# Another order of work in a software-pipelined attention and product-key expert layer

## The chip, the cores and the metric

One core of a Trainium2 chip runs the whole kernel. The metric is the device time of one execution in microseconds; lower is better. Times of single steps come from the profile of one execution.

## What is computed

One transformer layer on x of shape (16, 512, 128), float32, with a layer norm behind each half:

```python
x = layernorm(x + attention(x))     # 16 heads of 8, causal, q and k RMS-normed and rotated
x = layernorm(x + experts(x))       # product keys
# attention: qkv = x @ w_qkv.T; softmax(q k^T * 8**-0.5, causal) @ v; @ w_proj.T
# experts:
xn = rmsnorm(x) * norm_w
q = (xn @ w_q.T).reshape(b, t, 8, 2, 128)
sim1, sim2 = q[..., 0, :] @ keys0, q[..., 1, :] @ keys1      # 32 keys a side
s1, i1 = top_k(sim1, 8);  s2, i2 = top_k(sim2, 8)
fs, pk = top_k(s1[..., :, None] + s2[..., None, :], 8)       # of 64 pairs
fi = take_along(i1 * 32 + i2, pk)                            # 1024 experts
hidden = gelu(xn . expert_down[fi]) * relu(fs)
out = sum_k hidden_k * expert_up[fi_k]
```

## The kernel before

The 16 batches of 512 positions (four tiles of 128, `NT`) pass through a software pipeline. Each engine has its own program with one `iteration`, whose order is written out by hand, and all engines meet only at semaphores. In iteration b the batch `b` has its scores, exponentials and attention sums; `nxt` = b+1 is loaded, projected, normalised and rotated; `late` = b-1 gets its output projection, the first norm, similarities and selection; `older` = b-2 its expert weights; `oldest` = b-3 its expert outputs and the second norm. Iterations 3 to 14 are a loop; the ones ahead and behind leave out what has no batch. Where an expert is picked, no gather is made: the kernel computes `hid` for all 1024 experts (`hidden_products` L877, Gelu in `hidden` L553) and multiplies it with weights that come from one-hot matrices.

- Scores and exponentials. An iteration has 40 steps on TensorE and ScalarE, four groups of four heads with ten units each (`scores` L804, `exps` L609). The results alternate between two PSUM banks by the list `S_ORDER`, which also has the projections `v`, `xT`, `qk` and the transposed q and k (`Q`, `K`); a step in the list waits until what stood two places before is read. `attend` (L821) sums a group's values, 32 float32 products into OV; it waits for all ten exponentials of the group, and the first exponential of the next group waits for it, since `prob` has one buffer. `attended` (L625) copies OV, `transpose_o` (L835) turns it, `normalise_o` (L1134) divides by the sums. In the kernel before, `attend` of a group stands behind the second unit of the next one.
- q and k. `taken_qk` (L566) squares and copies them, `squares_summed` (L1081) sums, `rotate` (L434, GpSimd) turns them, `normalise` (L1096) multiplies them by their inverse roots. Then they are split into bfloat16 parts: `first_parts` (L580, ScalarE), `rests` (GpSimd), `second_parts` (ScalarE), `third_parts` (GpSimd), and `transpose_stack` (L759) and `transposed` (L598) bring them into `qT`, `kT` at four steps, `QK_STEPS`.
- Norms. `norm1_moments` (L1157) and `norm2` (L1181) take moments; `roots` (L1092) finds all inverse roots of q, k and both norms together, eleven dependent steps with one-hots in between; `norm1` (L1171) makes `yi`, which `transpose_yi` (L869) turns for `project_similarities` (L858), at `SIMS_STEPS`. ScalarE copies them in `similarities` (L546).
- Selection. `top_keys` (L1198) takes the maxima and their places of a tile (16 MAX8 and 16 FIND_INDEX8), `candidates` (GpSimd, L463) the sums, `top_pairs` (L1213) the best eight and a mask `gat`, `gather` (GpSimd, L489) multiplies the mask with the numbers, `turn_numbers` (L888) and `transpose_selection` (L900) turn them, `decode` (L1236) splits the experts' numbers. `top_pairs` of tile 0 waits for both rotations, as `gat` lies on their buffer.
- Weights. `one_hot` (L1258) writes 8 of 256 rows, 32 such instructions a batch; `weighted_one_hots` (L1271) makes a quarter of the other factor, `weights` (L909) multiplies 24 small products a part, 32 parts of 4 a chunk, and `apply_weights` (L1294) multiplies a chunk into `hid`. `expert_outputs` (L932) uses `hid`.

All operators on an engine are in order: a wait on one holds whatever is queued behind it.

## Time and profile before

| | us |
|---|---|
| median of three runs | 1940.49 (1939.04 to 1941.27) |
| profiled execution | 1938.47 |
| its span | 1936.6 |
| one pass of the loop, from 1003.40 | 112.64 |
| the next, from 1116.04 | 112.64 |

| busy over the span | TensorE | its weight loads | VectorE | ScalarE | GpSimd |
|---|---|---|---|---|---|
| us | 1430.0 | 1024.8 | 1385.7 | 920.6 | 630.4 |
| share | 74% | 53% | 72% | 48% | 33% |

The loop's twelve passes lie from 327 to 1678.6 us and repeat each other. "Idle" in brackets behind an instruction is the time its engine stood before it, and the name after the arrow is the instruction whose semaphore ended that. TensorE's ends are modelled; starts are not. PE is TensorE, PEld its weight loads, DVE VectorE, ACT ScalarE, POOL GpSimd.

### The profile page before, as it was taken

How to read it: one execution, taken by the hardware profiler on the slowest of the kernel's cores; microseconds unless marked ns; L12 is line 12 of the kernel's file. 1: busy time of each engine (PE TensorE's matmuls, PEld its weight loads, DVE VectorE, ACT ScalarE, POOL GpSimd, SP SyncE). 2: the span in 40 equal slices, each digit the busy share in tenths (PEclk: the TensorE clock that was granted, in tenths of full speed). 3: DMA queues.
4: the chain of work that ended last, by engine and by line, in shares of the span. 5: the costliest groups of instructions: out<-in, count | busy, mean ns of one | idle time of the engine just before them, and what ended most of it. 6: DMA issues, size and time to landing. Idle time of an engine off the chain costs nothing.

```text
span 1936.6 us, 55124 instructions
## 1 busy us (share of the span) xinstructions
PE 1430.0 (74%) x21008; PEld 1024.8 (53%) x21008; DVE 1385.7 (72%) x6568; ACT 920.6 (48%) x1502; POOL 630.4 (33%) x1024
## 2 busy tenths in 40 slices
PE   3665787777787777777777777787777778786757
PEld 2333455455565645555564555555455555555556
DVE  4217776777877677787767778876777887677885
ACT  1765544544555454455545445554544455441201
POOL 2315241432624143262414326241432624122220
PEclk7697978888897988889798888989888898987766
DMA  2000000000000000000000000000000000000000
GB/s 71 6 6 7 7 8 7 13 3 7 13 7 13 7 13 2 11 9 7 13 7 13 2 15 5 7 13 7 13 2 18 2 2 13 2 13 2 7 2 14
DMA packets 29989, 18.81 MB, mean 10 GB/s; under 512 B 1824, under 2 KB 29216, under 8 KB 29728
## 3 DMA queue, kind: packets, MB, share of 16 engines
q1 hardware_dynamic: 29728, 15.23, 2.8%
q8 instruction: 176, 2.88, 0.7%
q14 instruction: 85, 0.70, 0.1%
HBM read 11.04 MB, written 4.19 MB: 8 GB/s over the span
## 4 chain that ended last, share of the span: by engine, by line
DVE 37%; PE 34%; ACT 12%; issue 12%; POOL 3%; SPq 0%; DVEq 0%; ACTq 0%; DMA 0%; POOLq 0%
DVE onehot L1264 10%; PE OV L829 8%; PE G L937 6%; DVE topi L1210 5%; PE G L926 4%; PE S L815 4%; DVE psel L1226 3%; DVE topv L1204 3%; ACT prob L623 3%; PE F L895 2%; DVE whot L1289 2%; ACT kT_odd L607 2%; PE F L865 2%; DVE fsel L1221 2%; PE S L755 1%
## 5 line engine op out<-in xcount | busy, mean ns | idle before, releaser
L623 ACT ACTIVATE prob<-S 128x512 f32<-128x512 f32 x640 | 369.9, 601 | 718.7 <-PE S L817 380.0
L926 PE MATMUL G<-whot,onehot 128*128 128x16 bf16 x12288 | 387.7, 171 | 89.1 <-DVE hid L1302 88.8
L926 PEld LDWEIGHTS G<-whot,onehot 128*128 128x128 bf16 x12288 | 371.3, 99 | 133.7 <-issue 98.6
L1264 DVE TENSOR_TENSOR onehot<-lo_no,elo 128x1024 bf16<-128x1024 uint16 x512 | 388.4, 814 | 0.0
L815 PE MATMUL S<-qT,kT_even 128*128 128x512 bf16 (+3 forms) x512 | 157.2, 334 | 122.8 <-ACT kT_odd L607 51.2
L817 PE MATMUL S<-causal,ident_b 128*128 128x128 bf16 x1024 | 210.9, 239 | 0.0
L1204 DVE MAX8 topv<-sims 128x8 f32<-128x32 f32 x1024 | 101.2, 175 | 145.1 <-ACT sims L550 145.0
L829 PE MATMUL OV<-prob,vp 128*9 128x512 f32 (+3 forms) x2048 | 191.0, 524 | 0.7 <-ACT prob L623 0.7
L815 PE MATMUL S<-qT,kT_odd 128*128 128x256 bf16 (+3 forms) x512 | 158.4, 336 | 44.2 <-ACT prob L623 33.5
L502 POOL COPY y<-y_new 128x512 f32<-128x512 f32 x16 | 9.8, 611 | 500.7 <-DVE r L1188 442.5
L493 POOL TENSOR_TENSOR gat<-gat,cande 128x1280 f16<-128x1280 f16 x64 | 166.7, 2605 | 12.2 <-DVE gat L1232 12.2
L1210 DVE FIND_INDEX8 topi<-topv,sims 128x8 uint16<-128x32 f32 x1024 | 166.3, 185 | 1.9 <-issue 1.9
L815 PEld LDWEIGHTS S<-qT,kT_even 128*128 128x128 bf16 x512 | 52.3, 102 | 194.1 <-ACT kT_odd L607 60.4
L452 POOL TENSOR_TENSOR qk_u<-qk_r,stack 128x512 f32<-128x512 f32 x32 | 43.8, 1368 | 320.5 <-ACT stack L588 320.5
L895 PE MATMUL F<-ident_b,gat 128*64 128x128 bf16 x1280 | 102.1, 246 | 57.0 <-POOL gat L493 57.0
L937 PE MATMUL G<-up,hid 128*128 128x128 f32 x1024 | 127.9, 287 | 17.1 <-DVE hid L1302 17.1
L937 PEld LDWEIGHTS G<-up,hid 128*128 128x128 f32 x1024 | 125.3, 202 | 18.5 <-DVE hid L1302 17.6
L1138 DVE RECIPROCAL rden<-A 128x16 f32<-128x16 f32 x64 | 16.2, 253 | 162.6 <-PE A L839 162.6
L473 POOL TENSOR_SCALAR i<-topi 128x64 f16<-128x64 uint16 x128 | 53.5, 439 | 237.5 <-DVE topi L1210 237.3
L555 ACT ACTIVATE hid<-F 128x512 f32<-128x512 f32 x128 | 76.6, 598 | 102.8 <-PE F L885 102.8
L1289 DVE TENSOR_TENSOR whot<-hot_hi,wpart 128x1024 bf16<-128x1024 bf16 x192 | 123.4, 698 | 2.2
L817 PEld LDWEIGHTS S<-causal,ident_b 128*128 128x128 bf16 x1024 | 108.2, 106 | 28.9 <-issue 25.5
(134 smaller groups left out, 2587.0 us busy)
## 6 DMA issues: line engine op xcount, KB each, us to landing
xa<-in_L_attn_x SPq DMA_DIRECT2D x16, 256.0 KB, 2.8
xr<-in_L_attn_x SPq DMA_DIRECT2D x16, 256.0 KB, 2.8
out<-r SPq DMA_DIRECT2D x16, 256.0 KB, 2.3
onehot<-in_L_ffn_expert_down SPq DMA_DIRECT2D x1, 512.0 KB, 6.0
up<-in_L_ffn_expert_up SPq DMA_DIRECT2D x1, 512.0 KB, 7.2
onehot<-in_L_ffn_keys SPq DMA_DIRECT2D x1, 256.0 KB, 6.6
onehot<-in_L_attn_w_qkv SPq DMA_DIRECT2D x1, 192.0 KB, 4.9
onehot<-in_L_attn_w_proj SPq DMA_DIRECT2D x1, 64.0 KB, 4.8
```

What stands on the lines that cost most here:

```text
L493: pool.tensor_tensor(g, g, cande[:, t % 2].rearrange("p h c -> p c h").unsqueeze(3) .to_broadcast([P, NCAND, H, TOPK]), ALU.mult)\
L623: act.activation(dst, src, ACT.Exp, scale=SCALE).then_inc(exp_done.sem, 1)
L815: nc.tensor.matmul(bank[:, col:col + T - kc * P], pe_k, qT[:, j, kc * P:T], start=True, stop=False, skip_group_check=True)
L817: last = nc.tensor.matmul(bank[:, col:col + P], ident_b[:, :], causal[:, :], start=False, stop=True, skip_group_check=True)
L829: last = nc.tensor.matmul(OV[32 * i:32 * i + HD + 1, kc * P:T], vp[:, kc, 4 * g + i, :], prob[:, i, KC_AT[kc]:KC_AT[kc] + T - kc * P], sta ...
L895: last = nc.tensor.matmul(F_SEL[rows, t // 2 * P:(t // 2 + 1) * P], gat[:, t % 2, c].rearrange("p h k -> p (h k)"), ident_b[:, :], start=( ...
L926: last = nc.tensor.matmul(bank[:, 16 * i:16 * i + 16], onehot[:, row, :], whot[:, t, w_part, :], start=(w_part == 0), stop=(w_part == 2))
L937: last = nc.tensor.matmul(OUT[:, t * P:(t + 1) * P], hid[:, c, t * P:(t + 1) * P], up[:, c, :], start=(c == 0), stop=(c == NHI - 1))
L1204: last = dve.max(out=topv[:, t, s, h, :], in_=sims[:, t % 2, s, h, :])
L1210: last = dve.max_index(topi[:, t, s, h, :], topv[:, t, s, h, :], sims[:, t % 2, s, h, :])
L1264: dve.tensor_tensor(onehot[:, row:row + 8, :].rearrange("p t (c i) -> p t c i", i=2), lo, e, ALU.is_equal)
L1289: last = dve.tensor_tensor(whot[:, t0:t0 + 64, part, :].rearrange("p t (c i) -> p t c i", i=2), hot, wpart[:, part, pair, t0:t0 + 64].unsq ...
```

## The change

Only order and two signals change; each instruction is still there, with the same shapes.

- TensorE: `attend` of a group stands at the end of that group's last step, and for group 3 ahead of the next iteration's first scores, with `project_v` and `transpose_x` behind it. `expert_outputs` moves from steps 2 and 3 to 4, around `project_out`. `SIMS_STEPS`, `NUMBER_STEPS`, `SELECTION_STEP`, `QK_STEPS` and the two steps without weights change.
- ScalarE follows: copies of OV at steps 9, 19, 29; similarities right behind steps 8, 9, 14, 17; the parts of q and k at 13, 17, 20, 21.
- VectorE: the first norm's moments ahead of the second's, the squares and one weighted set ahead of both, one-hots 16 to 19 in the roots, 20 to 23 behind; two `top_keys` ahead of the first `normalise`, the second `normalise` behind the first `top_pairs`; chunks 4 and 5 weighted one place earlier, one-hots 28 to 31 last.
- GpSimd: waits for `yi` before it rotates; the rotations, candidates and gather are interleaved.
- `rows_done` is new: TensorE waits at part 28 for the last one-hots, which no longer stand ahead of `hot_done`.

```diff
--- before.py
+++ after.py
@@ -256,6 +256,7 @@
         dec = signal("dec", 4, 4)
         hi_done = signal("hi_done", 4)
         hot_done = signal("hot_done", 4)
+        rows_done = signal("rows_done", 1)
         g_ready = signal("g_ready", 8)
         g_free = signal("g_free", 8, 2)
         ffn_ready = signal("ffn_ready", NT)
@@ -281,13 +282,13 @@
         S_ORDER = [("scores", n) for n in range(NG * UNITS)]
-        QK_STEPS = [25, 29, 33, 39]
+        QK_STEPS = [27, 31, 35, 39]
         for g in reversed(range(NG)):
             at = S_ORDER.index(("scores", QK_STEPS[g])) + 1
             S_ORDER[at:at] = [("Q", g), ("K", g)]
-        for step, two in ((3, [("qk", 0), ("qk", 1)]), (1, [("v", 0), ("xT", 0)])):
-            at = S_ORDER.index(("scores", step)) + 1
-            S_ORDER[at:at] = two
+        at = S_ORDER.index(("scores", 3)) + 1
+        S_ORDER[at:at] = [("qk", 0), ("qk", 1)]
+        S_ORDER[0:0] = [("v", 0), ("xT", 0)]
         S_READ = {"scores": exp_done, "v": v_done, "xT": xT_done, "qk": sq_done, "Q": qT_done, "K": kT_done}
         def pass_wait(eng):
@@ -344,10 +345,10 @@
-        SIMS_STEPS = [9, 11, 17, 21]
-        NUMBER_STEPS = [22, 27, 32, 35]
-        SELECTION_STEP = 36
-        WEIGHT_STEPS = [n for n in range(5, 39) if n not in (21, 31)]
+        SIMS_STEPS = [8, 9, 13, 15]
+        NUMBER_STEPS = [22, 28, 34, 35]
+        SELECTION_STEP = 35
+        WEIGHT_STEPS = [n for n in range(5, 39) if n not in (19, 29)]
         block = ctx.enter_context(nc.Block())
@@ -505,20 +506,27 @@
                 if older is not None:
                     keep_rows(older)
+                if late is not None:
+
+                    pool.wait_ge(yi_done.sem, yi_done.value(late, 1))
                 if nxt is not None:
                     rotate(nxt, 0)
+                if late is not None:
+                    candidates(late, 0)
+                if nxt is not None:
                     rotate(nxt, 1)
+                if late is not None:
+                    candidates(late, 1)
+                    gather(late, 0)
+                if nxt is not None:
                     rests(nxt, 0)
                     rests(nxt, 1)
                 if late is not None:
-                    candidates(late, 0)
+                    candidates(late, 2)
                 if nxt is not None:
                     third_parts(nxt, 0)
                     third_parts(nxt, 1)
                 if late is not None:
-                    candidates(late, 1)
-                    gather(late, 0)
-                    candidates(late, 2)
                     gather(late, 1)
                     candidates(late, 3)
                     gather(late, 2)
@@ -647,16 +655,15 @@
             def iteration(b, late, older, oldest, nxt):
+                if late is not None:
+                    attended(late, NG - 1)
+                if b is not None:
+                    taken_v(b)
+                if nxt is not None:
+                    taken_x(nxt)
                 for n in range(NG * UNITS):
                     if b is not None:
                         exps(b, n // UNITS, [n % UNITS])
-                    if n == 1:
-                        if late is not None:
-                            attended(late, NG - 1)
-                        if b is not None:
-                            taken_v(b)
-                        if nxt is not None:
-                            taken_x(nxt)
                     if n == 3:
                         if nxt is not None:
                             taken_qk(nxt, 0)
@@ -666,33 +673,24 @@
                     if n == 4 and older is not None:
                         for c in range(NHI):
                             hidden(older, c)
-                    if n == 9 and late is not None:
+                    if n == 7 and late is not None:
                         normed(late)
-                    if n == 10:
-                        if late is not None:
-                            similarities(late, 0)
-                            norm1_rows(late)
-                        if oldest is not None:
-                            norm2_rows(oldest)
-                    if n == 12:
-                        if b is not None:
-                            attended(b, 0)
-                        if late is not None:
-                            similarities(late, 1)
-                    if nxt is not None and n in (13, 14):
-                        first_parts(nxt, n - 13)
-                    if nxt is not None and n in (16, 17):
-                        second_parts(nxt, n - 16)
-                    if n == 19 and late is not None:
-                        similarities(late, 2)
-                    if n == 22 and b is not None:
-                        attended(b, 1)
-                    if n == 23 and late is not None:
-                        similarities(late, 3)
-                    if n == 32 and b is not None:
-                        attended(b, 2)
+                    if late is not None and n in (8, 9):
+                        similarities(late, n - 8)
+                    if nxt is not None and n in (13, 17):
+                        first_parts(nxt, (n - 13) // 4)
+                    if n == 12 and late is not None:
+                        norm1_rows(late)
+                    if n == 13 and oldest is not None:
+                        norm2_rows(oldest)
+                    if nxt is not None and n in (20, 21):
+                        second_parts(nxt, n - 20)
+                    if late is not None and n in (14, 17):
+                        similarities(late, 2 + (n - 14) // 3)
                     if nxt is not None and n in QK_STEPS:
                         transposed(nxt, QK_STEPS.index(n))
+                    if b is not None and n in (9, 19, 29):
+                        attended(b, n // UNITS)
             iteration(None, None, None, None, 0)
             iteration(0, None, None, None, 1)
@@ -914,6 +912,9 @@
                 if part % 8 == 0:
                     pe.wait_ge(hot_done.sem, hot_done.value(b, part // 8 + 1))
+                if part == 28:
+
+                    pe.wait_ge(rows_done.sem, rows_done.value(b, 1))
                 if quarter == 0:
                     pe.wait_ge(g_free.sem, g_free.value(b, chunk - 1))
@@ -942,42 +943,40 @@
+                if late is not None:
+                    attend(late, NG - 1)
+                if b is not None:
+                    project_v(b, nxt)
+                if nxt is not None:
+                    transpose_x(nxt, b)
                 for step in range(NG * UNITS):
                     g, u = step // UNITS, step % UNITS
                     if b is not None:
                         scores(b, g, [u], nxt)
-                        if u == 1 and g:
-                            attend(b, g - 1)
-                    if step == 1:
-                        if late is not None:
-                            attend(late, NG - 1)
-                        if b is not None:
-                            project_v(b, nxt)
-                        if nxt is not None:
-                            transpose_x(nxt, b)
-                    if step == 2:
-                        if oldest is not None:
-                            expert_outputs(oldest, range(2))
-                        if late is not None:
-                            transpose_o(late, NG - 1)
+                    if step == 1 and late is not None:
+                        transpose_o(late, NG - 1)
                     if step == 3:
                         if nxt is not None:
                             project_qk(nxt, 0, b)
                             project_qk(nxt, 1, b)
-                        if oldest is not None:
-                            expert_outputs(oldest, range(2, NT))
                         if late is not None:
                             turn_outputs(late)
                     if step == 4:
+                        if oldest is not None:
+                            expert_outputs(oldest, range(2))
                         if late is not None:
                             project_out(late)
+                        if oldest is not None:
+                            expert_outputs(oldest, range(2, NT))
                         if older is not None:
                             hidden_products(older)
+                    if nxt is not None and step in QK_STEPS:
+                        transpose_stack(nxt, QK_STEPS.index(step), b)
                     if older is not None and step in WEIGHT_STEPS:
                         weights(older, WEIGHT_STEPS.index(step))
-                    if step == 8 and late is not None:
+                    if step == 7 and late is not None:
                         transpose_yi(late)
-                    if b is not None and u == 3 and g:
+                    if b is not None and u == 1 and g:
                         transpose_o(b, g - 1)
                     if late is not None and step in SIMS_STEPS:
                         project_similarities(late, SIMS_STEPS.index(step))
@@ -985,8 +984,8 @@
                         turn_numbers(late, NUMBER_STEPS.index(step))
                     if late is not None and step == SELECTION_STEP:
                         transpose_selection(late)
-                    if nxt is not None and step in QK_STEPS:
-                        transpose_stack(nxt, QK_STEPS.index(step), b)
+                    if b is not None and u == UNITS - 1 and g < NG - 1:
+                        attend(b, g)
                 if nxt is not None and shifted:
                     shift_by_maxima(nxt, b)
...
+                return dve.tensor_tensor(onehot[:, row:row + 8, :].rearrange("p t (c i) -> p t c i", i=2), lo, e,
+                                         ALU.is_equal)
@@ -1308,19 +1307,19 @@
                 hot = (lambda first, last: range(first, last)) if older is not None else (lambda first, last: ())
                 if oldest is not None:
                     apply_weights(oldest, 7)
-                one_hots(hot(8, 14))
+                one_hots(hot(8, 10))
                 if late is not None:
                     normalise_o(late, NG - 1)
+                one_hots(hot(10, 14))
+                if nxt is not None:
+                    squares_summed(nxt)
                 one_hots(hot(14, 16))
                 if older is not None:
                     weighted_one_hots(older, 1)
+                if late is not None:
+                    norm1_moments(late)
                 if oldest is not None:
                     norm2(oldest)
-                one_hots(hot(16, 20))
-                if nxt is not None:
-                    squares_summed(nxt)
-                if late is not None:
-                    norm1_moments(late)
                 if nxt is not None:
                     dve.wait_ge(qsum_done.sem, qsum_done.value(nxt, 1))
                 if oldest is not None:
@@ -1328,53 +1327,59 @@
                 first = AT_QK if nxt is not None else AT_NORM1 if late is not None else AT_NORM2
                 last = AT_NORM2 if oldest is not None else AT_NORM1 if late is not None else AT_QK
                 if nxt is not None or late is not None or oldest is not None:
-                    roots(turn, slice(first.start, last.stop), hot(20, 24))
+                    roots(turn, slice(first.start, last.stop), hot(16, 20))
                 else:
-                    one_hots(hot(20, 24))
+                    one_hots(hot(16, 20))
                 if late is not None:
                     norm1(late)
                 if oldest is not None:
                     norm2_shift(oldest)
+                one_hots(hot(20, 23))
                 if older is not None:
                     apply_weights(older, 0)
+                one_hots(hot(23, 24))
+                if late is not None:
+                    top_keys(late, 0)
+                    top_keys(late, 1)
                 if nxt is not None:
                     normalise(nxt, 0)
-                    normalise(nxt, 1)
-                if late is not None:
-                    top_keys(late, 0)
                 if older is not None:
                     apply_weights(older, 1)
-                    weighted_one_hots(older, 2)
                 if b is not None:
                     normalise_o(b, 0)
-                if late is not None:
-                    top_keys(late, 1)
+                if older is not None:
+                    weighted_one_hots(older, 2)
+                if late is not None:
                     top_pairs(late, 0)
+                if nxt is not None:
+                    normalise(nxt, 1)
                 if older is not None:
                     apply_weights(older, 2)
-                one_hots(hot(24, 28))
                 if late is not None:
                     top_keys(late, 2)
                     top_pairs(late, 1)
                 if older is not None:
                     apply_weights(older, 3)
-                one_hots(hot(28, 32))
+                one_hots(hot(24, 28))
+                if late is not None:
+                    top_keys(late, 3)
                 if older is not None:
                     weighted_one_hots(older, 3)
                 if b is not None:
                     normalise_o(b, 1)
-                if late is not None:
-                    top_keys(late, 3)
+                if older is not None:
+                    apply_weights(older, 4)
+                if late is not None:
                     top_pairs(late, 2)
                 if older is not None:
-                    apply_weights(older, 4)
+                    apply_weights(older, 5)
                 if late is not None:
                     top_pairs(late, 3)
-                if older is not None:
-                    apply_weights(older, 5)
                 if b is not None:
                     normalise_o(b, 2)
                 if older is not None:
+                    one_hots(range(28, 31))
+                    one_hot(31).then_inc(rows_done.sem, 1)
                     apply_weights(older, 6)
                 if late is not None:
                     decode(late)
```

## Rows read from the trace of the kernel before

**Rows 1.** the page: busy time and share of each engine; the chain that ended last.
```profile
PE 1430.0 (74%) x21008; PEld 1024.8 (53%) x21008; DVE 1385.7 (72%) x6568; ACT 920.6 (48%) x1502; POOL 630.4 (33%) x1024
...
DVE 37%; PE 34%; ACT 12%; issue 12%; POOL 3%; SPq 0%; DVEq 0%; ACTq 0%; DMA 0%; POOLq 0%
```

**Rows 2.** by stretch: length, PE, PEld, DVE, ACT, POOL busy, granted clock, DMA share, GB/s.
```profile
1003.40:1116.04 112.64, 87.02 (x1311) 62.65 (x1312) 85.10 (x407) 57.52 (x95) 39.78 (x63) 0.86 0.03 9
1087.50:1094.00 6.50, 5.75 (x60) 2.12 (x60) 3.47 (x26) 0.58 (x2) 4.99 (x2) 0.57 0.00 0
133.40:217.20 83.80, 52.99 (x464) 30.15 (x464) 53.66 (x353) 48.39 (x80) 36.05 (x63) 0.86 0.03 7
217.20:326.80 109.60, 81.30 (x1248) 55.65 (x1247) 85.22 (x393) 56.22 (x90) 37.82 (x62) 0.83 0.02 7
1678.30:1781.00 102.70, 77.45 (x1228) 55.97 (x1228) 78.36 (x400) 39.48 (x70) 24.53 (x45) 0.84 0.02 7
1781.00:1875.00 94.00, 58.49 (x958) 47.19 (x958) 78.06 (x397) 12.69 (x23) 24.58 (x45) 0.65 0.01 4
```

**Rows 3.** VectorE's waits in the loop pass 1003.4 to 1116.04; us, times, longest.
```profile
DVE topv L1204 <- ACT sims L550: 9.5, 1, 9.5
DVE rden L1138 <- PE A L839: 7.5, 2, 6.7
DVE hot_hi L1246 <- PE F L905: 3.7, 1, 3.7
DVE hid L1302 <- PE G L926: 2.1, 1, 2.1
DVE r L1188 <- PE G L937: 1.5, 1, 1.5
```

**Rows 4.** TensorE's timeline in that pass: start, us, line, tiles, count, idle before.
```profile
1009.87 3.73 PE L937 MATMUL G<-up,hid 128*128 128x128 f32 x32
...
1015.78 7.32 PE L885 MATMUL F<-xn,downT 128*128 128x512 f32 x16
...
1033.47 1.11 PE L874 MATMUL F<-ident,yi 128*128 128x128 f32 x4 [5.79 <-DVE yi L1174]
...
1059.09 2.34 PE L829 MATMUL OV<-prob,vp 128*9 128x512 f32 x32
...
1067.40 2.34 PE L895 MATMUL F<-ident_b,gat 128*64 128x128 bf16 x20 [4.00 <-POOL gat L493]
...
1087.52 0.79 PE L926 MATMUL G<-whot,onehot 128*128 128x16 bf16 x24 [3.68 <-DVE hid L1302]
...
1088.89 4.37 PE L829 MATMUL OV<-prob,vp 128*9 128x512 f32 x32
```

**Rows 5.** ScalarE's timeline, the first exponential behind attention sums 0.
```profile
1043.57 0.60 ACT L623 ACTIVATE prob<-S 128x512 f32<-128x512 f32 x1 [7.14 <-PE OV L829]
```

**Rows 6.** VectorE's timeline in the same pass.
```profile
1003.52 3.69 DVE L1264 TENSOR_TENSOR onehot<-lo_no,elo 128x1024 bf16<-128x1024 uint16 x6
...
1023.51 1.23 DVE L1264 TENSOR_TENSOR onehot<-lo_no,elo 128x1024 bf16<-128x1024 uint16 x1
...
1031.54 0.31 DVE L1076 SCALAR_TENSOR_TENSOR qk_t<-qk_t,qk_rs 128x140 f32<-128x140 f32 x1
...
1032.22 1.11 DVE L1174 TENSOR_SCALAR yi<-xr,mv,qk_rs 128x128 f32<-128x128 f32 x4
...
1063.71 1.57 DVE L1204 MAX8 topv<-sims 128x8 f32<-128x32 f32 x16
...
1068.02 0.73 DVE L1221 MAX8 fsel<-candv 128x8 f32<-128x20 f32 x8
...
1071.56 4.93 DVE L1264 TENSOR_TENSOR onehot<-lo_no,elo 128x1024 bf16<-128x1024 uint16 x4
...
1104.96 0.69 DVE L1246 CAST hot_hi<-F 128x512 uint16<-128x512 f32 x1 [3.72 <-PE F L905]
```

**Rows 7.** GpSimd's timeline: gather 1.
```profile
1071.53 2.60 POOL L493 TENSOR_TENSOR gat<-gat,cande 128x1280 f16<-128x1280 f16 x1
```

6 lines of the change are left out of this document (2 added, 4 removed).

## Prediction

> **What bounds the kernel now.** First the page's shares: TensorE is busy 74% and VectorE 72%, and the chain that ended last runs through VectorE 37%, TensorE 34%, ScalarE 12% [rows 1]. No engine is full, two take turns. Then the table by stretches: one pass of the loop takes 112.64 us, the next the same to 0.01; twelve passes are 1352 of the 1936.6 us span. VectorE works 85.10 us of a pass, TensorE 87.02 [rows 2], so it idles 27.5. Then its waits within one pass [rows 3]: 9.5 us for the first similarities, 7.5 in front of the attention sums' reciprocals, 3.7 for the selection (decode), 2.1 and 1.5 for TensorE; 24.3 in all. The other 3.2 are gaps of at most 0.3. Last TensorE's timeline [rows 4]: it stands 5.79 us for yi, 4.00 for the first gather, 3.68 for the weighting of a chunk. The two wait for each other: roots end late, yi is late, TensorE stands; then ScalarE's queue holds the first similarities behind an exponential that waits 7.14 us for the attention sums [rows 5], and VectorE stands 9.5.
>
> **Before yi.** I count a pass from the start of decode on VectorE (1104.96; 992.32 in the pass before). In the kernel before, yi ends at 1033.33, so at 41.0 [rows 6]. The new order has in front of it: the same work less four one-hots (8 to 19 instead of 8 to 23), at 0.60 each (six in 3.69): -2.4. The waits of 0.8 (reciprocal) and 1.5 (r <- expert outputs) are covered: norm2 now stands behind six one-hots, the squares, a weighted set and the first moments. Reckoned through, VectorE wants the outputs at 23.5, and TensorE has them at about 22.0 (attend group 3 4.6 to 6.9, projections of v, q, k to 12.8, two blocks of 3.7 with the projection between, from 13.8): -2.3. The roots took from 1023.1, one step ahead of the one-hot of 1023.51, to 1032.22: 9.1 us, beside the rotations on GpSimd. These are now held by the new wait for yi, so 11 root steps at 0.34 (two of them from 1031.54 to 1032.22) and 4 one-hots at 0.60 make 6.2 to 6.3: -2.8 [rows 6], and the small instruction before them about -0.5. yi is done at 33.0. TensorE comes to it at 32.7 (from 22.0: eight products 7.3, five to seven with weights 2.8, one exponential 0.8 late after the gelus). The stall of 5.8 goes, and nothing takes its place but some 0.5.
>
> **From yi to the end.** Three one-hots, a weighting and one more follow. The rotations now run exactly here. A one-hot beside such an operation took 1.23 [rows 6], so about 3.5 for three, 0.6, and 1.2, and the maxima begin at 38.5. Similarities 0 are copied by about 36.9: steps 8 and 9 come before ScalarE meets the group boundary. In the kernel before they began at 1044.81, that is 52.5. From there to the next decode are 60.1 us, of which 12.5 are waits (6.7, 2.1, 3.7), so 47.6 of work. To this come the two normalisations (1.3), which stood ahead; the moved weighted set and first normalisation beside the second rotation and candidates (by the same row, 0.6 for each of two or three collisions: 1.4, ends 0 and 3); and one-hots 24 to 31. Of these four took 4.93 as their first waited for a gather of 2.60 [rows 6, 7], the other four 2.7. Now 24 to 27 meet the third parts and gather 1 (6.1 by that row), 28 to 31 stand right behind gather 3 (4.5): together +3.0. 47.6 + 1.3 + 1.4 + 3.0 = 53.3.
>
> **New waits.** (1) TensorE waits at part 28 for rows 28 to 31. Behind it are part 28 (0.6), the last turned numbers (1.3 quick, 2.3 at the lower clock) and the selection (0.3); decode waits for that, and only one weighting (0.6) hides it: 1.7 at the least, up to 2.9. I take 2.2. (2) ScalarE meets first_parts at step 13, while normalisation 0 stands behind maxima 0 and 1 on VectorE, 4.3 each (1063.71 to 1068.02 [rows 6]): 38.5 + 8.7 + 0.7, done at 47.9, and ScalarE comes there at 45.1. Queued behind: norm2's rows (1.6), exponential 14. TensorE stands some 4.0 at step 16. At step 17 the same with the second half, done at 55.2 to 56.6; exponentials 18 and 19 are behind it, and attend group 1 starts only at 58.4, after 3.7 of standing. This is TensorE's slack (at step 16 it was 4 us ahead), but after such gaps the clock is low: after the 3.68 gap the granted clock was 0.57 over the next 6.5 us (most of it at 1.2 GHz) and the sums took 4.37 us instead of 2.34 [rows 2, 4]. Then chunk 3 is late for VectorE by 1.9; I take 0.5 as part of it falls into the locks already counted (ends 0 and 1.9). (3) attend now stands ahead of the next scores: at steps 19 and 29 nothing is left between the last exponential and the sums, about 0.9 each, against the 0.8 behind each boundary that disappears: nothing in sum. (4) GpSimd's wait for yi: rotations start some 14 us later than the squares, and top pairs 0 waits for both. They end at about 50 to 51, VectorE comes at 51.5. Cover is thin: if lost, 1 us. The wait ahead of the selection goes from 3.7 to the 2.2 above. Other moved steps (transposes of outputs, stacks at 27, 31, 35, 39, similarities at 13 and 15, scores after v) lie beside VectorE's work; stacks in front of a weights' part hide 0.6 of their copy.
>
> **Sum.** 38.5 + 53.3 + 2.2 + 0.5 = 94.5 us a pass, VectorE bound, 18.1 less; 12 passes: 217. Pass 2 (109.6, the same without norm2): -17. Pass 15 (102.7, VectorE 78.4 busy, no rotations): 78.4 + 3.2 gaps + 3 locks + 3 waits = 87.6: -15. Pass 16 (94.0, 78.1 busy, no scores): about 85: -9. Pass 1 (83.8, 53.7 busy): it has the same late similarities: -9. The first two passes and the last two: nothing. Together 267. 1938.47 (span 1936.6 and 1.9 around it) - 267 = 1671; the median of the runs is 2.0 above: **1673**.
>
> **A rule of the skill.** The trace: four one-hots that were issued 0.03 us behind the gather of 1071.53 took 4.93, where four take 2.5 alone; the loss of 2.5 is the gather's 2.60 [rows 6, 7]. So the one that starts second waits. The Trainium skill, page "SBUF — State Buffer", section "SBUF: two separate sides", says just this of VectorE instructions with two SBUF inputs: an exclusive lock for the whole instruction. It speaks against this change, which moves rotations beside one-hots. By it, if VectorE came second each time, the second rival below would be the result.
>
> **Rivals.**
> - Packed (0.14): gather 1 and the third parts miss the one-hots, and TensorE keeps its clock. Then the pass is 38.5 + 50.3 + 1.7 less 1.5 at the first rows: 89 to 91. 12 x 22.6 + 60 = 331: 1609. For: six one-hots without a neighbour took 3.69. Against: gather 3 starts right ahead of row 28 by order.
> - More locks and a low clock (0.20): VectorE is second each time: four rows at a wait of 0.7 to 1.2 beside rotations, four operations of the weighted set the same, and the full 1.9 of chunk 3 and 2.9 of decode. 5 us more: 99.5. 12 x 13.1 + 40 = 197: 1743. By the skill's page named above, that is the case where GpSimd always holds the lock.
> - TensorE stays the bound (0.09): the two new stands (4.0 + 3.7), the wait at part 28 and the low clock after each (2.0 for one attend, 0.2 to 0.3 a step) take the place of 5.8 + 4.0 + 3.7: 110 us a pass, about 1900. Against it: similarities 13 us earlier on VectorE, which TensorE's stands alone can't give back.
> - The other side (0.05): ScalarE's queue at steps 13 and 17. If normalisation 0 and the second were each 10 us later than reckoned, 20 us would be added to the ring, and 94.5 becomes 114.5, over 112.6. Point from which it decides: 9 us each, normalisation 0 at 57 or later. 14 passes of 1.9 more: 1966. For it: two maxima (4.4 each), the candidates, a rotation and the top pairs are all in the ring that leads to it.
> - No net change (0.02): both effects equal, 1940.
>
> **How the numbers follow.** The forecast has 0.50 (92 to 97 us a pass, 1640 to 1705). The range 1605 to 1765 takes in most of the packed case and the locks: 0.8. A measurement of this kernel can tell 0.2%, some 4 us. Faster: 0.50 + 0.14 + 0.20 + 0.09 = 0.93; same 0.02; slower 0.05.
>
> **What would show it.** Right: VectorE busy 90% or more of the loop; no wait of VectorE for similarities over 1 us; TensorE's wait for yi under 1.5; two new waits of the stack copies on ScalarE for the normalised q and k, of 2 to 4 us each, with TensorE waiting for exponentials at steps 16 and 19; the roots done in about 6.3 us; one-hots 28 to 31 with one of about 2.5 to 3; rows to decode about 2.2. Wrong: VectorE idle over 10 us a pass, above all in front of top pairs 0 (rotations late), a weighting (chunk late) or the reciprocals; or rows 20 to 22 far over 1.2 each.

## The result, and the profile after

| | before | after |
|---|---|---|
| median | 1940.35 us | 1626.3 us (1625.77 to 1626.44, four runs) |
| profiled execution, its span | 1938.47, 1936.6 | 1626.17, 1624.4 |
| one pass of the loop, mean of the twelve | 112.6 us | 90.4 us |

The ratio is 0.838, 95% interval 0.837 to 0.840: 314 us less, where 267 were forecast. The page of the changed kernel, the row that answers to [rows 1]:

```profile
PE 1353.0 (83%) x21008; PEld 973.5 (60%) x21008; DVE 1358.7 (84%) x6568; ACT 926.0 (57%) x1502; POOL 665.0 (41%) x1024
```

By stretches (columns as in [rows 2]): one pass, the low-clock stretch behind the longest stand, then passes 1, 2, 15 and 16:

```profile
930.00:1020.30 90.30, 80.78 (x1311) 58.60 (x1312) 83.78 (x406) 57.85 (x95) 42.25 (x63) 0.94 0.04 11
978.40:985.00 6.60, 6.59 (x92) 3.27 (x93) 5.02 (x49) 2.23 (x5) 4.78 (x13) 0.71 0.00 0
131.60:208.00 76.40, 54.05 (x462) 30.37 (x462) 47.55 (x347) 49.01 (x82) 35.88 (x63) 0.84 0.03 8
208.00:296.60 88.60, 74.78 (x1246) 52.06 (x1246) 81.01 (x396) 56.41 (x92) 41.79 (x62) 0.92 0.03 8
1381.80:1474.30 92.50, 78.87 (x1266) 56.41 (x1258) 77.75 (x400) 39.74 (x70) 24.90 (x45) 0.91 0.03 8
1474.30:1559.30 85.00, 54.41 (x956) 44.71 (x954) 75.21 (x392) 12.70 (x23) 25.03 (x45) 0.72 0.02 5
```

VectorE is busy 83.8 of 90.3 us, 93% where it was 76%. Its work hardly changed (85.1 to 83.8); what went is idle time, 27.5 to 6.5 us. Its waits in the pass (us, times, longest; compare [rows 3]):

```profile
DVE hot_hi L1245 <- PE F L903: 1.9, 1, 1.9
DVE hid L1301 <- PE G L927: 1.6, 2, 1.4
...
DVE r L1187 <- DVE qk_ms L1166: 0.3, 1, 0.3
DVE topv L1203 <- ACT sims L558: 0.2, 1, 0.2
```

The 9.5 us for the similarities are 0.2, the reciprocals wait no more, decode 1.9 instead of 3.7. VectorE's timeline, counted like the prediction from the start of decode at 921.20:

```profile
921.20 0.69 DVE L1245 CAST hot_hi<-F 128x512 uint16<-128x512 f32 x1 [1.86 <-PE F L903]
...
946.76 0.23 DVE L1068 TENSOR_SCALAR qk_rs<-qk_ms 128x140 int32<-128x140 int32 x1
...
952.38 1.11 DVE L1173 TENSOR_SCALAR yi<-xr,mv,qk_rs 128x128 f32<-128x128 f32 x4
...
953.56 1.89 DVE L1263 TENSOR_TENSOR onehot<-lo_no,elo 128x1024 bf16<-128x1024 uint16 x3
...
957.48 1.58 DVE L1203 MAX8 topv<-sims 128x8 f32<-128x32 f32 x16 [0.21 <-ACT sims L558]
```

The roots run from 946.76 to 952.38, 5.6 us where they took 9.1. yi ends at 953.49, so at 32.3 (33.0 forecast, 41.0 before), and the first maxima begin at 36.3 (38.5 forecast, 52.5 before). Twelve passes at 22.2 us are 266 of the gain; pass 2 gives 21, pass 15 10, pass 16 9, pass 1 7; the two ends together are about 2 us longer than before.

### The profile page after: what moved, and what is told of

It reads as the page before. It is cut to its first block, busy times and chain, and to the rows that moved or that the text cites. A ratio compares the mean times of both kernels' runs of the same rounds, so it can differ in the third digit from the quotient of the medians.

```text
span 1624.4 us, 55167 instructions
## 1 busy us (share of the span) xinstructions
PE 1353.0 (83%) x21008; PEld 973.5 (60%) x21008; DVE 1358.7 (84%) x6568; ACT 926.0 (57%) x1502; POOL 665.0 (41%) x1024
## 3 DMA queue, kind: packets, MB, share of 16 engines
HBM read 11.04 MB, written 4.19 MB: 9 GB/s over the span
## 4 chain that ended last, share of the span: by engine, by line
PE 41%; DVE 36%; ACT 9%; issue 8%; POOL 5%; SPq 1%; DVEq 0%; DMA 0%; ACTq 0%; POOLq 0%
DVE onehot L1263 10%; PE G L938 7%; PE OV L827 7%; PE F L883 7%; DVE topi L1209 6%; PE G L927 6%; DVE psel L1225 4%; DVE whot L1288 3%; PE S L813 3%; DVE topv L1203 3%; ACT prob L631 3%; DVE fsel L1220 2%; DVE hid L1301 2%; PE S L753 2%; PE F L893 2%
## 5 line engine op out<-in xcount | busy, mean ns | idle before, releaser
L494 POOL TENSOR_TENSOR gat<-gat,cande 128x1280 f16<-128x1280 f16 x64 | 178.6, 2790 | 75.9 <-DVE gat L1231 75.9
L815 PE MATMUL S<-causal,ident_b 128*128 128x128 bf16 x1024 | 200.9, 229 | 0.0
L813 PE MATMUL S<-qT,kT_even 128*128 128x512 bf16 (+3 forms) x512 | 145.1, 312 | 53.7 <-ACT prob L631 45.0
L827 PEld LDWEIGHTS OV<-prob,vp 128*9 128x9 f32 x2048 | 54.9, 99 | 198.2 <-issue 107.2
L441 POOL TENSOR_TENSOR gat<-qk_r,cosw 128x256 f32<-128x256 f32 x64 | 75.4, 1179 | 231.5 <-DVE yi L1173 178.8
L1288 DVE TENSOR_TENSOR whot<-hot_hi,wpart 128x1024 bf16<-128x1024 bf16 x192 | 131.6, 739 | 2.2
L638 ACT ACTIVATE oT<-OV 128x512 f32<-128x512 f32 x64 | 38.2, 597 | 155.2 <-PE OV L827 155.2
L883 PE MATMUL F<-xn,downT 128*128 128x512 f32 x256 | 117.2, 611 | 0.0
L474 POOL TENSOR_SCALAR i<-topi 128x64 f16<-128x64 uint16 x128 | 64.6, 524 | 124.9 <-DVE topi L1209 124.8
L1301 DVE TENSOR_TENSOR hid<-G,hid 128x512 f32<-128x512 f32 x128 | 87.5, 684 | 33.7 <-PE G L927 33.7
```

Source lines behind the costliest of these rows:

```text
L494: pool.tensor_tensor(g, g, cande[:, t % 2].rearrange("p h c -> p c h").unsqueeze(3) .to_broadcast([P, NCAND, H, TOPK]), ALU.mult)\
L813: nc.tensor.matmul(bank[:, col:col + T - kc * P], pe_k, qT[:, j, kc * P:T], start=True, stop=False, skip_group_check=True)
L815: last = nc.tensor.matmul(bank[:, col:col + P], ident_b[:, :], causal[:, :], start=False, stop=True, skip_group_check=True)
L827: last = nc.tensor.matmul(OV[32 * i:32 * i + HD + 1, kc * P:T], vp[:, kc, 4 * g + i, :], prob[:, i, KC_AT[kc]:KC_AT[kc] + T - kc * P], sta ...
L883: nc.tensor.matmul(bank_hid(c)[:, :], downT[:, c * P:(c + 1) * P], xn[:, :], start=True, stop=True)\
L1288: last = dve.tensor_tensor(whot[:, t0:t0 + 64, part, :].rearrange("p t (c i) -> p t c i", i=2), hot, wpart[:, part, pair, t0:t0 + 64].unsq ...
```

## The experiments

Times are medians; a "pass" is the mean of eight passes of the loop in the profiled execution, from one copy of x to the next. (That execution was the fastest of te_longer's, 1630.8 us, and the slowest of ve_gp_new's and both's, 1957.7 and 1623.1.)

| kernel | us | ratio to before, 95% | pass |
|---|---|---|---|
| before | 1940 | | 112.6 |
| changed | 1626.3 | 0.838 (0.837 to 0.840) | 90.4 |
| te_sc_new | 1890.7 | 0.974 (0.972 to 0.976) | 109.7 |
| ve_gp_new | 1951.9 | 1.006 (1.003 to 1.009) | 112.8 |
| sc_steps_mended | 1841.9 | 0.948 (0.946 to 0.951) | 105.8 |
| sims_first | 1928.1 | 0.994 (0.992 to 0.996) | 112.6 |
| no_yi_wait | 1668.3 | 0.859 (0.857 to 0.861) | 93.9 |
| norm2_first | 1677.5 | 0.865 (0.863 to 0.867) | 94.7 |
| attend_back | 1659.0 | 0.855 (0.854 to 0.857) | 92.2 |
| norm_q_first | 1621.1 | 0.837 (0.834 to 0.839) | 90.1 |
| rows_early | 1616.7 | 0.834 (0.832 to 0.835) | 90.2 |
| both | 1615.2 | 0.832 (0.830 to 0.834) | 90.5 |
| ve_longer | 1639.1 | 0.847 (0.844 to 0.849) | 91.4 |
| te_longer | 1636.1 | 0.844 (0.842 to 0.846) | 91.5 |

**Half the engines in the new order.** te_sc_new takes the programs of TensorE and ScalarE from the changed kernel and those of VectorE and GpSimd from the one before; the last one-hots signal `rows_done`:

```diff
-                one_hots(hot(28, 32))
+                one_hots(hot(28, 31))
+                if older is not None:
+                    one_hot(31).then_inc(rows_done.sem, 1)
```

> Half of the change: TensorE and ScalarE in the new order, VectorE and GpSimd in the old one (rows_done still signalled with the last one-hots). My theory (both halves are needed, because the two engines wait for each other in a ring): similarities are early, but the roots still take about 9 us beside the rotations and norm2 stands first and waits some 3 us for the expert outputs, so yi is at 41 to 44 us of a pass and TensorE stands 6 to 10 us for it; a pass takes 98 to 106 us, the kernel 1750 to 1860. Rival (the gain is in TensorE's and ScalarE's order alone): at most 1690 us.

It took 1890.7 us, less gain than I expected (a pass of 109.7, not 98 to 106). TensorE's timeline, its stand for yi, and VectorE's, its stand for the expert outputs (last bracket: idle before, and what ended it):

```profile
788.50 1.11 PE L865 MATMUL F<-ident,yi 128*128 128x128 f32 x4 [8.96 <-DVE yi L1166]
```

```profile
768.88 0.69 DVE L1180 TENSOR_TENSOR r<-G,y 128x512 f32<-128x512 f32 x1 [5.67 <-PE G L931]
```

The signs are as expected: similarities are early, but VectorE's norm2 stands in front and waits 5.7 us for outputs that TensorE now makes later, and TensorE waits 9.0 for yi. A part of the loss is not that ring, though. VectorE also stands 5.0 us ahead of top pairs 0 (0.3 before), and TensorE 7.7 for the first gather (4.0 before):

```profile
DVE fsel L1213 <- issue: 5.0, 1, 5.0
```

```profile
PE F L886 <- POOL gat L494: 7.7, 1, 7.7
```

```profile
809.05 1.15 POOL L453 TENSOR_TENSOR qk_u<-qk_r,stack 128x512 f32<-128x512 f32 x1 [4.47 <-ACT stack L589]
```

GpSimd's old order has the candidates behind `rests`, and these wait for ScalarE's first parts, which the new ScalarE program makes at steps 13 and 17 instead of 13 and 14. No run tried the new TensorE and ScalarE with GpSimd's order mended, so how much of the missing gain is this and how much the ring stays open.

ve_gp_new is the other half, the new VectorE and GpSimd with the old TensorE and ScalarE. One line is added to the old TensorE program:

```diff
+                if part == 28:
+                    pe.wait_ge(rows_done.sem, rows_done.value(b, 1))
```

> The other half: VectorE and GpSimd in the new order, TensorE (with the one wait for the last one-hots that the order needs) and ScalarE in the old one. My theory: yi is at about 33 us of a pass and TensorE's stand of 5.8 us for it goes, but the first similarities are still queued on ScalarE behind the exponential that waits for attention sums 0, so VectorE stands 5 to 8 us for them; a pass takes 98 to 105 us, the kernel 1740 to 1850. Rival (VectorE's order alone makes the gain): at most 1690 us. Second rival (without early similarities it gives nothing): 1900 us or more.

1951.9 us: a little slower than before; the second rival. VectorE and ScalarE, timelines:

```profile
832.73 1.59 DVE L1215 MAX8 topv<-sims 128x8 f32<-128x32 f32 x16 [7.58 <-ACT sims L558]
...
858.91 1.59 DVE L1215 MAX8 topv<-sims 128x8 f32<-128x32 f32 x16 [7.57 <-ACT sims L558]
```

```profile
843.32 0.84 ACT L595 ACTIVATE stack<-qk_r 128x768 bf16<-128x768 f32 x1 [5.27 <-DVE qk_r L1112]
...
850.78 0.84 ACT L595 ACTIVATE stack<-qk_r 128x768 bf16<-128x768 f32 x1 [5.40 <-DVE qk_r L1112]
```

yi was early here (TensorE waited 0.4 us for it), as my theory had it. But the old ScalarE program has the first similarities behind the exponential of the next group (7.6 us), and takes the parts of q and k at steps 13 and 14, which VectorE's new order brings later: 5.3 and 5.4 us of standing, and similarities 2 are queued behind that, so that VectorE stands 7.6 us again. This is the prediction's rival on the other side, ScalarE's queue; it does decide if ScalarE's steps aren't moved too.

To see whether that queue was the cause, sc_steps_mended changes ScalarE alone in that kernel:

```diff
                     if n == 9 and late is not None:
                         normed(late)
+                        similarities(late, 0)
...
-                        if late is not None:
-                            similarities(late, 0)
-                            norm1_rows(late)
+                        if late is not None:
+                            norm1_rows(late)
...
-                    if nxt is not None and n in (13, 14):
-                        first_parts(nxt, n - 13)
-                    if nxt is not None and n in (16, 17):
-                        second_parts(nxt, n - 16)
+                    if nxt is not None and n in (13, 17):
+                        first_parts(nxt, (n - 13) // 4)
+                    if nxt is not None and n in (20, 21):
+                        second_parts(nxt, n - 20)
```

> VectorE and GpSimd in the new order, TensorE in the old one as in the run that gained nothing (1952 us), but on ScalarE alone the first similarities stand ahead of the first exponential of group 1, and the parts of q and k at steps 13, 17, 20, 21 as in the change instead of 13, 14, 16, 17. My theory (that run failed by ScalarE's queue: 7.6 us for the similarities, 5.3 and 5.4 us for the normalised q and k, and 7.6 again for similarities behind them): VectorE's first stand falls under 3 us and a pass to 100 to 106 us, 1780 to 1870 us. Rival (the old place of the attention sums and expert outputs on TensorE is what holds it): 1900 us or more.

1841.9 us, 110 us less for the place of a few ScalarE instructions; a pass fell from 112.8 to 105.8. Time and pass are in the range of my theory, and the first stand fell from 7.6 to 2.9 us, just under the 3 that I had named. But two more stands for similarities follow it, of 4.7 and 2.6 us:

```profile
774.12 1.59 DVE L1215 MAX8 topv<-sims 128x8 f32<-128x32 f32 x16 [2.93 <-ACT sims L558]
```

```profile
DVE topv L1215 <- ACT sims L558: 10.2, 3, 4.7
DVE rden L1149 <- PE A L847: 8.7, 2, 5.5
```

TensorE still makes the similarities at steps 9, 11, 17 and 21. The remaining 15 us a pass to the changed kernel are thus TensorE's order and ScalarE's with it. The parts don't add: TensorE and ScalarE alone win 50 us, VectorE and GpSimd alone lose 11, and all together win 314.

**One wait alone.** sims_first moves, in the kernel before, only the copy of the first similarities on ScalarE (the first two hunks of the diff above).

> The kernel before with one ScalarE copy moved: the first similarities ahead of the first exponential of group 1 instead of behind it. My theory: VectorE's stand of 9.5 us for them falls to 2 to 4 us, and 3 to 6 us a pass are gained: 1865 to 1900 us. Rival (the wait only changes its name, as TensorE's late yi sets the pass): within 0.5% of the kernel before.

My theory fell. The stand of 9.5 us for the similarities fell to 4.1, and a pass takes 112.6 as before (111.5 and 113.8 in turn); the 12 us won lie in the passes ahead of and behind the loop. VectorE's waits in one such pass:

```profile
DVE rden L1138 <- PE A L839: 8.3, 3, 6.8
DVE hid L1302 <- PE G L926: 4.3, 2, 2.2
DVE topv L1204 <- ACT sims L550: 4.1, 1, 4.1
...
DVE fsel L1221 <- issue: 2.1, 1, 2.1
```

The time went to the reciprocals (8.3, 7.5 before), the weightings (4.3, 2.1 before) and the first top pairs (2.1, 0.3 before), with TensorE's stands of 5.8, 4.0 and 3.7 us unchanged: the wait changed its name, the rival's words. (The kernel as a whole gained 0.6%, just more than the rival's 0.5%, all of it outside the loop.)

**GpSimd's wait for yi.** no_yi_wait is the changed kernel without it:

```diff
-                if late is not None:
-
-                    pool.wait_ge(yi_done.sem, yi_done.value(late, 1))
```

> The changed kernel without GpSimd's wait for yi: the rotation of the first half runs beside the roots again. My theory (the wait keeps the shared operands free for the roots): the roots take 7.5 to 9.5 us instead of 5.6, yi is 2 to 4 us later in a pass, of which up to 1 us comes back at the one-hots behind it; 1 to 3 us a pass, 1640 to 1670 us. Rival (the wait is only ordering, the collisions move from one place to another): within 0.4% of the changed kernel's 1626.

1668.3 us, 42 us more, 3.5 a pass. VectorE's timeline, first step of the roots, first one-hot in them, yi, the one-hots behind:

```profile
690.49 0.72 DVE L1065 TENSOR_SCALAR qk_rs<-qk_ms 128x140 int32<-128x140 int32 x1
...
691.13 1.23 DVE L1260 TENSOR_TENSOR onehot<-lo_no,elo 128x1024 bf16<-128x1024 uint16 x1
...
698.23 1.11 DVE L1170 TENSOR_SCALAR yi<-xr,mv,qk_rs 128x128 f32<-128x128 f32 x4
...
699.41 1.89 DVE L1260 TENSOR_TENSOR onehot<-lo_no,elo 128x1024 bf16<-128x1024 uint16 x3
```

The roots take 7.7 us (690.49 to 698.23) instead of 5.6, one-hots in them 1.23 instead of 0.68. Behind yi the one-hots take 1.89, as in the changed kernel: nothing comes back there. VectorE's wait for the first similarities is 1.3 us where it was 0.2, which with the 2.1 of the roots makes up most of the 3.5. So the added wait, which makes GpSimd idle, is worth 42 us.

**The order of the norms.** norm2_first puts VectorE's norm2 back ahead of the squares and the first norm's moments:

```diff
-                if nxt is not None:
-                    squares_summed(nxt)
                 one_hots(hot(14, 16))
                 if older is not None:
                     weighted_one_hots(older, 1)
-                if late is not None:
-                    norm1_moments(late)
                 if oldest is not None:
                     norm2(oldest)
+                if nxt is not None:
+                    squares_summed(nxt)
+                if late is not None:
+                    norm1_moments(late)
```

> The changed kernel with VectorE's norm2 again ahead of the squares and the first norm's moments, all else new. My theory (the change's order covers the expert outputs): VectorE waits 1.5 to 4 us for the outputs, yi is that much later, and so is the pass: 1640 to 1675 us. Rival (the order of the norms doesn't matter, the stand is absorbed): within 0.4% of 1626 us.

1677.5 us, just over the top of my range, 4.3 us a pass more. VectorE's waits, and TensorE's:

```profile
DVE r L1187 <- PE G L938: 3.3, 1, 3.3
DVE hid L1301 <- PE G L927: 2.1, 2, 1.6
```

```profile
PE F L872 <- DVE yi L1173: 2.6, 1, 2.6
```

3.3 us for the outputs (0.3 in the changed kernel, for another reason) come through whole, TensorE stands 2.6 for yi, and VectorE then 1.3 for the first similarities (0.2): 4.1 of the 4.3.

**The attention sums.** attend_back puts them, the projection of v and the transposes of x back behind the second unit of the next group, on both engines. ScalarE's copies of OV and the transposes of them follow, to steps 12, 22, 32 and to the fourth unit. A part of the edit:

```diff
-                if late is not None:
-                    attend(late, NG - 1)
-                if b is not None:
-                    project_v(b, nxt)
-                if nxt is not None:
-                    transpose_x(nxt, b)
                 for step in range(NG * UNITS):
...
+                    if b is not None and u == 1 and g:
+                        attend(b, g - 1)
+                    if step == 1:
+                        if late is not None:
+                            attend(late, NG - 1)
+                        if b is not None:
+                            project_v(b, nxt)
+                        if nxt is not None:
+                            transpose_x(nxt, b)
...
-                    if b is not None and u == UNITS - 1 and g < NG - 1:
-                        attend(b, g)
```

> The changed kernel with the attention sums (and the projection of v and the transposes of x) back behind the second unit of the next group, on TensorE and ScalarE; all else new. My theory (the prediction put their move at nothing in sum: 0.9 us ahead of two boundaries against 0.8 behind each): within 1.5 us a pass, 1608 to 1646 us. Rival (the move of the sums is a main part of the gain, since ScalarE's exponentials and copies no longer queue behind them): 1670 us or more.

1659.0 us lies between the two: the move is worth 33 us, not nothing and not a main part. VectorE's waits in a pass:

```profile
DVE rden L1140 <- PE A L839: 2.9, 2, 2.4
...
DVE r L1190 <- PE G L940: 0.9, 1, 0.9
```

The reciprocals wait 2.9 us and norm2 0.9, where the changed kernel has none and 0.3: transposes of the sums come two steps later and the start of a pass is late. No stand for exponentials ahead of the sums is left here, and TensorE's granted clock was 0.98 (0.92 in a pass of the changed kernel); the time was lost all the same. TensorE's idle time as a whole grew, from 9 to 13 us a pass.

**Is TensorE's standing slack?** (Slack is time that an engine can lose without the pass growing.) norm_q_first puts the first normalisation between the first two maxima:

```diff
                 if late is not None:
                     top_keys(late, 0)
-                    top_keys(late, 1)
                 if nxt is not None:
                     normalise(nxt, 0)
+                if late is not None:
+                    top_keys(late, 1)
```

> The changed kernel with the first normalisation of q and k between the first two maxima on VectorE, so that ScalarE finds it done at step 13. My theory (VectorE sets the pass, TensorE's stand of 2.3 us at step 16 is slack): the stand goes and the time stays within 0.6%, 1616 to 1636 us. Rival (TensorE's stand and the low clock behind it are on the path): 1600 us or less. Second rival (the first rotation isn't done in time, VectorE waits for it): 1640 or more.

1621.1 us, 0.3% less, which the intervals (0.834 to 0.839 and 0.837 to 0.840) don't tell apart. TensorE's waits in a pass:

```profile
PE OV L827 <- ACT prob L631: 5.8, 2, 5.1
PE S L813 <- ACT prob L631: 1.8, 2, 1.0
```

The wait of 2.3 us at step 16 is at most 1.0, and that ahead of the sums grew from 3.1 to 5.1: TensorE had only met the second half's block earlier. The first stand is slack: taken away, it gives nothing. The second is not shown to be. It grew by 2 us and the pass did not, but no run takes it away, and what VectorE still waits for right behind it is chunk 3.

**The lock behind the gather.** rows_early moves one-hots 28 to 31:

```diff
                 if older is not None:
                     apply_weights(older, 4)
+                    one_hots(range(28, 31))
+                    one_hot(31).then_inc(rows_done.sem, 1)
                 if late is not None:
                     top_pairs(late, 2)
...
-                    one_hots(range(28, 31))
-                    one_hot(31).then_inc(rows_done.sem, 1)
                     apply_weights(older, 6)
```

> The changed kernel with one-hots 28 to 31 between the weighting of chunk 4 and top pairs 2, away from gather 3. My theory: the loss of about 2 us behind the gather goes, but decode's wait for the selection grows from 1.9 to 3.0 to 3.8 us, since now top pairs 3, gather 3 and the turned numbers are what is late: 0 to 1 us a pass less, 1612 to 1627 us. Rival (the lock is the only thing in the way): 1604 us or less. Second rival (the selection's chain counts more than the lock): 1635 or more.

1616.7 us, 9.6 less, as expected. VectorE's one-hots 24 to 27 and 28 to 31, and its wait for the selection:

```profile
709.64 4.26 DVE L1263 TENSOR_TENSOR onehot<-lo_no,elo 128x1024 bf16<-128x1024 uint16 x4
...
721.90 2.62 DVE L1263 TENSOR_TENSOR onehot<-lo_no,elo 128x1024 bf16<-128x1024 uint16 x4
```

```profile
DVE hot_hi L1245 <- PE F L903: 3.4, 1, 3.4
```

The four took 2.62 us instead of 4.64, and decode waits 3.4 instead of 1.9: 2.0 won, 1.5 given back. The twelve passes of the loop give about half of the 9.6 us; most of the rest is pass 15, 90.5 us where it took 93.7.

both has the two edits.

> The changed kernel with both edits that were a little faster alone: one-hots 28 to 31 ahead of top pairs 2 (1616.7 us) and the first normalisation between the first two maxima (1621.1 us). My theory (one takes time off VectorE, the other only shortens a stand of TensorE and the low clock behind it): 1606 to 1616 us, faster than both kernels. Rival (the second adds nothing): 1616 to 1620 us.

1615.2 us, with runs from 1610 to 1623: faster than both kernels, but not to be told from rows_early. The second edit adds nothing that can be measured.

**Who sets the pass?** ve_longer puts three instructions of 0.6 us more on VectorE, and te_longer makes the first turned numbers twice on TensorE (1.1 us more by its trace, 1.25 by my estimate):

```diff
                 one_hots(hot(20, 23))
+                for n in range(3 if older is not None else 0):
+                    dve.tensor_reduce(extra[:, n, :], downT[:, n % 2 * 512:n % 2 * 512 + 512]
+                                      .rearrange("p (g d) -> p g d", d=HD), AX.X, ALU.add)
```

> The changed kernel with three more instructions on VectorE behind one-hots 20 to 22 in each pass with weights (sums over constant values into a spare tile, 0.6 us each; nothing reads them). My theory (VectorE sets the pass): all but the 0.4 us of its two short waits right behind come through, 1.4 to 1.8 us in 16 passes, 1645 to 1660 us. Rival (TensorE sets it as much, the extra time falls into VectorE's 6.5 us of idle a pass): at most 1634 us.

```diff
-                for c in range(NCAND):
+                for c in [*range(NCAND), *range(NCAND)] if t == 0 else range(NCAND):
```

> The changed kernel with the first turned numbers made twice on TensorE (20 more small products at step 22, about 1.25 us a pass, where it did not stand). My theory (TensorE has slack there, VectorE sets the pass): within 0.5% of 1626 us, 1618 to 1634. Rival (TensorE sets the pass from there on): 16 passes of 1.2, 1642 us or more.

Neither theory nor rival. ve_longer is 12.8 us slower of 29 added (its runs spread from 1638 to 1650), te_longer 9.8 of some 18 (1631 to 1639). One pass of the changed kernel, of ve_longer and of te_longer:

```profile
658.20:748.80 90.60, 81.72 (x1310) 59.06 (x1310) 83.48 (x407) 57.94 (x95) 42.24 (x63) 0.92 0.04 11
```

```profile
660.30:752.10 91.80, 80.75 (x1311) 58.52 (x1312) 85.49 (x411) 58.15 (x96) 42.09 (x63) 0.94 0.04 11
```

```profile
659.90:751.60 91.70, 81.49 (x1331) 59.59 (x1332) 83.23 (x407) 58.24 (x96) 42.25 (x63) 0.96 0.04 11
```

About half of either addition comes through in the time of the kernel, but within the loop, by the mean of its twelve passes, 1.1 of 1.8 us for VectorE and 0.9 of 1.1 for TensorE, most of it. TensorE's addition reaches VectorE as a longer wait for weighted chunks, 1.7 us on average over ten passes of the changed kernel and 2.6 here. VectorE is busiest, but it does not set the pass alone; both engines are in the ring.

## Why the prediction was right, and where it was off

- What bounds the kernel: right. Two engines took turns, the idle time was the price, and no work had to go. te_sc_new and ve_gp_new are in keeping with it, but neither is a clean test: each half also met a third engine in an order that did not fit (GpSimd's candidates, ScalarE's copies), and mending one of the two gave 110 us.
- Before yi: right to 0.7 us (32.3 for 33.0). The covered waits are shown by norm2_first (3.3 us return when norm2 stands first), the roots' share by no_yi_wait (7.7 to 5.6). I had put the roots at 6.3, with 0.34 for each of eleven steps. That is the time from start to start where one step waits for the last; the four steps with a one-hot queued behind them took 0.14 to 0.22, as the first, of 946.76, whose one-hot started 0.15 us later:

```profile
946.91 0.68 DVE L1263 TENSOR_TENSOR onehot<-lo_no,elo 128x1024 bf16<-128x1024 uint16 x1
```
- From yi to the maxima: the term for three one-hots beside the rotation (3.5) was mis-sized; they took 1.89. GpSimd's rotation came second:

```profile
953.67 2.37 POOL L441 TENSOR_TENSOR gat<-qk_r,cosw 128x256 f32<-128x256 f32 x1 [7.81 <-DVE yi L1173]
...
898.51 3.06 POOL L494 TENSOR_TENSOR gat<-gat,cande 128x1280 f16<-128x1280 f16 x1
```

The rotation started at 953.67, 0.11 us after the one-hot of 953.56, and took 2.37 where it takes 0.73 alone; VectorE's three one-hots ran through, as in every other pass of the loop (2.29 to 2.37). I had taken the row of 1023.51, a one-hot that came second, for all of them. One-hots 24 to 27, which I put at 6.1, took 3.97 (2.5 alone) for another reason: they met GpSimd's third parts, and there the two engines took turns. The one-hots took 0.74, 1.15, 1.15 and 1.16 us, and three of the third parts 1.1 each, where the first took 0.67; gather 1 behind them took 3.06 instead of 2.61. One-hots 28 to 31, by order behind gather 3, took 4.64 (4.5 forecast):

```profile
895.28 1.12 POOL L461 TENSOR_TENSOR stack<-qk_u,stack 128x256 bf16<-128x256 f32 x1
```

```profile
895.79 1.15 DVE L1263 TENSOR_TENSOR onehot<-lo_no,elo 128x1024 bf16<-128x1024 uint16 x1
```

```profile
895.13 3.97 DVE L1263 TENSOR_TENSOR onehot<-lo_no,elo 128x1024 bf16<-128x1024 uint16 x4
...
914.10 4.64 DVE L1263 TENSOR_TENSOR onehot<-lo_no,elo 128x1024 bf16<-128x1024 uint16 x4
```

The Trainium skill, page "SBUF — State Buffer", section "SBUF: two separate sides", says that when a VectorE instruction with two SBUF inputs meets a GpSimd instruction, whichever starts first holds the pair of ports that the two engines share for its whole length, and the other blocks fully. The third parts and the gathers agree. The rotation doesn't quite: by the trace two of the three one-hots started after it (954.16 and 954.76) and still ran first, at 0.7 us each, and no run shows why. The rival in which VectorE always comes second did not come true, nor did its opposite: in one pass nine of VectorE's instructions are lengthened, by 5.6 us in all, and 17 of GpSimd's, by 8.0. In a pass of the kernel before, VectorE's loss was 5.7. So the new order did not take the collisions away; it moved them, out of the roots and behind yi.
- From the maxima to decode: forecast 53.3 and 2.7 of waits; measured 54.0. 1.8 of the difference are one-hots 24 to 27 (4.26 us in this pass). Chunk 3's wait was sized at 0.5; it was 1.4 to 2.0. Decode's wait was 1.9 (2.2 forecast).
- The new waits on ScalarE are where they were put, at the normalised q and k, and TensorE's behind them; they are shorter than the 2 to 4 us forecast for each:

```profile
967.41 0.84 ACT L595 ACTIVATE stack<-qk_r 128x768 bf16<-128x768 f32 x1 [1.19 <-DVE qk_r L1100]
...
975.33 0.84 ACT L595 ACTIVATE stack<-qk_r 128x768 bf16<-128x768 f32 x1 [1.85 <-DVE qk_r L1100]
```

```profile
971.06 0.34 PE L813 MATMUL S<-qT,kT_even 128*128 128x384 bf16 x1 [2.30 <-ACT prob L631]
...
978.41 4.19 PE L827 MATMUL OV<-prob,vp 128*9 128x512 f32 x32 [3.12 <-ACT prob L631]
```

ScalarE stood 1.2 and 1.9 us, TensorE 2.3 (4.0 forecast) and 3.1 (3.7 forecast), after which the sums took 4.19 us at a granted clock of 0.71 over 978.4 to 985. That the first is slack is shown by norm_q_first. The second isn't: the slow sums stand ahead of chunk 3, for which VectorE waits 1.4 to 2.0 us here. The prediction had this chain, but took only 0.5 of it.
- The move of the attention sums: put at nothing, worth 33 us (attend_back). I had counted only TensorE's stand at each boundary, and not that the transposed sums, and all at the start of a pass, come earlier for VectorE.
- "VectorE bound": half right. Of what is added to VectorE or to TensorE about half comes through, within the loop more of TensorE's than of VectorE's. The sum by VectorE's work still gave the right size since it is busy 93%.
- The sum: 94.5 us a pass forecast, 90.4 measured. That is outside the forecast's own 92 to 97 (and 1626 outside its 1640 to 1705), and inside the 89 to 91 of the packed rival, whose conditions did not hold: one-hots 24 to 27 did meet the third parts, and TensorE's clock did fall. The stated range takes in 1626 by its width. With 12 passes the 4.1 us are 49, about the whole difference of 1673 to 1626: 0.7 before yi, 1.5 from there to the maxima, 2.0 behind. Pass 15 won 10, not 15; pass 2 21, not 17.
- The rival on the other side did not come, but its mechanism is real: in ve_gp_new ScalarE stood 5.3 and 5.4 us at just that place.

Open: why three kernels with VectorE's waits in different places (before, sims_first, ve_gp_new) have passes of 112.6 to 112.8 us. TensorE's low clock behind each stand takes time, but no run separates that from the order. Open too: which of the two engines goes next when both stand at the lock, and what TensorE's second stand costs.

## What to carry to other kernels

Where two engines each idle a quarter of a loop and wait for each other, count each one's work from a fixed point of a pass and follow both orders: here the pass came near the busier engine's work plus its real waits (94.5 reckoned, 90.4 measured), and moving one engine's program without the others' can win nothing (50 us were won by one half, 11 lost by the other, and 314 won by both). A copy or a conversion on a third engine that stands ahead of its turn holds everything behind it, so its step must move with the one that feeds it. An engine that runs ahead may be worth holding back: a wait that made GpSimd idle until yi was done won 42 us.

## What the hardware showed that I had not expected

- The lock of VectorE and GpSimd does not always go the same way. Three one-hots in a row kept it, 1.89 us for the three, while the rotation took 2.37 instead of 0.73; four others in a row took turns with the third parts and each took up to 1.16 instead of 0.68, and one behind a gather took 2.84.
- A stand taken out of a pass need not shorten it at all: 9.5 to 4.1 us with a pass of 112.6 both times. And time added to either of two engines came through by about half: 12.8 of 29 us, 9.8 of some 18.
